# Attention's value product with its operands exchanged: values stationary, four heads in four column strips, output transposed

## The chip, the cores and the metric

The kernel runs on one core of one Trainium2 chip. The metric is the device time of one execution in microseconds (us): 1140.92 us is the median of three runs (1137.62 to 1145.13). The engines are named as in the profile: PE is TensorE's matmuls, PEld its weight loads, DVE is VectorE, ACT ScalarE, POOL GpSimd and SP SyncE.

## The reference, cut to what matters

Two layers, each an attention with context (16 batches of 128 tokens, width 256, 16 heads of 16) and a mixture of experts that picks 2 of 16 (layer 0) or 2 of 8 (layer 1). All values are float32. In each layer the attention is, for every batch:

```
qh = heads(norm(x) @ Wq + bq); kh = heads(ctx @ Wk + bk); vh = heads(ctx @ Wv + bv)
scores = q k^T / 4                 (causal mask in layer 0, masked query rows in layer 1)
attn   = softmax(scores)           (over the 128 keys)
out    = (attn @ vh) joined over heads, (128, 256)
x      = x + tanh(g) * (out @ Wo + bo)
```

The change is in `attn @ vh` and in what leads from it to `@ Wo`.

## The kernel before, in words

A tile is one batch: 128 tokens on the partitions. `attend(t)` is written out for every engine, and its order is the order of the engine's queue; counters (semaphores) tie the queues together, and `need(engine, counter, value)` is a wait. The work of several tiles is interleaved by hand: while tile t has its scores and its softmax, tile t-1 has its last value product, its division and its output projection, tile t+1 its projections, t-2 its second normalisation, t-3 to t-5 the routing of tokens to experts. The loop runs over 21 steps in each layer. The times of the stages are in the profile section.

The heads are taken in four groups g of four. For a group PE makes the scores of four heads at once (L1200, 128 x 512, in layer 0 with the causal mask added by L1204), DVE takes the row maxima (L806) and scales them (L811, L813), ACT takes the exponentials (L643), PE turns the four 128 x 128 blocks round (`turn_p`, L1212), ACT copies them to `probT` (L650), and PE multiplies them by the values (`weigh_v`, L1225). There each head is one matmul: its turned probabilities (128 keys x 128 queries) are the stationary operand, and the moving one has 17 columns: 16 values and a column of ones, which gives the row sum. So the 16 heads of a tile fill 272 columns of `bank[4]`, with the queries on the partitions.

`divide` on DVE takes the reciprocal of the 16 row sums (L834, 128 x 16) and multiplies (L837). `turn_o` on PE (L1238, two transposes) turns the result round, `oT_copy` on ACT (L656) brings it to SBUF, and `proj_o` (L1246) multiplies it by Wo. `residual` (L843, L845) adds it to x. In PE's order of a step stand: score 0; the transposes of the normalised x of t+1 (`turn_x`, L1154) and its value projection (L1180); routing (L1266 to L1277); `turn_p` 3 and `weigh_v` 2 of t-1; score 1; key projection (L1171); `turn_p` 0; `weigh_v` 3 of t-1; score 2; query projection (L1190); `turn_o` of t-1; `turn_p` 1, `weigh_v` 0, score 3; `proj_o` of t-1; `turn_p` 2, `weigh_v` 1. In DVE's order `divide` of t-1 stands between the maxima of group 1 and of group 2. POOL runs beside them: the power of the variance (L496), a part of the keys' blocks (L502), and the low parts of the experts' weights (L508), which are made ahead.

## Time and profile before

| | |
|---|---|
| median of three runs | 1140.92 us (1137.62 to 1145.13) |
| span of the profiled execution, first to last instruction | 1135.2 us |
| time of the profiled execution beside its span | not recorded apart; the span is 5.7 us under the median of the runs |
| attention of layer 0, first to last division | 39 to 274 us |
| attention of layer 1, first to last division | 483 to 776 us |
| experts, layer 0 / layer 1 | about 320 to 450 / about 800 to 1100 us |
| busy, whole span | PE 81%, PEld 64%, DVE 58%, ACT 49%, POOL 32% |

All times within the profile are from the span's start. A float32 matmul shows as two records, each with its own weight load: 1024 records at L1225 are 512 matmuls. The end of a matmul's record is modelled, and records overlap, so the pace is read from starts and from the chain of waits (the chain of work that ended last, followed back), not from busy time.

### The profile page before, as it was taken

Reading aid. Unit: us, or ns where it says so; the run is one execution under the profiler, and the core shown is the slowest. Engines: PE = TensorE matmul, PEld = TensorE weight load, DVE = VectorE, ACT = ScalarE, POOL = GpSimd, SP = SyncE. Lnnn points to the kernel's source line nnn. Section 1 sums busy time; section 2 is a strip of 40 time slices with the busy share of each in tenths; the row PEclk is TensorE's granted clock in tenths of the full one; section 3 lists DMA queues with packets and bytes.
Section 4 is the critical chain, followed back from the end, with each engine's and each line's share of the span. In section 5 each row is a group of like instructions: output and inputs, shape, how many; then the busy total and the mean of one; then the engine's idle time right before and its main releaser. Section 6 shows DMA issues by size and latency. Waiting matters only on the chain.

```text
span 1135.2 us, 26126 instructions
## 1 busy us (share of the span) xinstructions
PE 920.6 (81%) x7417; PEld 731.3 (64%) x7441; DVE 663.6 (58%) x1683; ACT 551.5 (49%) x1434; POOL 365.7 (32%) x359
## 2 busy tenths in 40 slices
PE   5998888996498885889888878885699999999920
PEld 3777676775486654567777657663577777777710
DVE  3678778786654444486777677675433334443323
ACT  3666656665234552575666566573233443333300
POOL 1335445454400001554564665565100000000046
PEclk9999899998699998797867787786799999999975
DMA  3121221221313443222222222120311111111034
GB/s 115 57 84 45 66 68 53 65 66 70 114 32 111 128 131 119 72 82 79 65 90 89 72 90 88 63 98 38 131 39 38 37 37 37 37 37 37 20 102 139
DMA packets 58764, 83.48 MB, mean 74 GB/s; under 512 B 8272, under 2 KB 49872, under 8 KB 58320
## 3 DMA queue, kind: packets, MB, share of 16 engines
q1 hardware_dynamic: 51984, 65.42, 18.0%
q0 software_dynamic: 6144, 16.79, 4.4%
q8 instruction: 32, 0.52, 0.2%
q10 hardware_dynamic: 576, 0.52, 0.1%
q14 instruction: 28, 0.23, 0.1%
HBM read 54.39 MB, written 28.31 MB: 73 GB/s over the span
## 4 chain that ended last, share of the span: by engine, by line
PE 56%; DVE 20%; issue 13%; POOL 5%; ACT 2%; DMA 2%; SPq 1%; another core or an unknown queue 1%; DVEq 0%; POOLq 0%; ACTq 0%
PE bank L1397 14%; PE bank L1410 13%; PE bank L1200 7%; PE bank L1225 5%; DVE work L795 5%; DVE work L806 3%; PE bank L1212 3%; POOL work L583 3%; PE bank L1385 2%; PE bank L1180 2%; PE bank L1171 2%; PE bank L1190 2%; PE bank L1154 2%; PE bank L1362 1%; PE bank L1277 1%
## 5 line engine op out<-in xcount | busy, mean ns | idle before, releaser
L1397 PE MATMUL bank<-work,arena 128*128 128x128 bf16 x2496 | 223.1, 224 | 0.0
L1397 PEld LDWEIGHTS bank<-work,arena 128*128 x2496 | 183.1, 98 | 28.8 <-issue 6.7
L1410 PE MATMUL bank<-arena,work 128*128 x1104 | 181.2, 275 | 6.5 <-DVE work L1112 1.1
L1200 PE MATMUL bank<-work 128*128 128x512 f32 x256 | 156.0, 694 | 1.4 <-ACT work L607 1.4
L643 ACT ACTIVATE work<-bank,work,qscale 128x128 f32<-128x128 f32 x256 | 96.8, 465 | 88.8 <-DVE work L813 79.0
L1225 PEld LDWEIGHTS bank<-work 128*128 128x128 f32 x1024 | 137.5, 209 | 0.6 <-ACT work L650 0.5
L806 DVE TENSOR_REDUCE work<-bank 128x4 f32<-128x512 f32 x128 | 88.2, 689 | 84.8 <-PE bank L1200 40.8
L1225 PE MATMUL bank<-work 128*128 128x17 f32 x1024 | 134.8, 265 | 0.4 <-ACT work L650 0.4
L583 POOL DMA_INDIRECT work<-y,slot x32 | 31.3, 977 | 298.0 <-DMA y<-work 288.6
L756 ACT ACTIVATE work<-bank,b 128x128 f32<-128x128 f32 x160 | 45.7, 368 | 164.1 <-PE bank L1397 164.1
L643 ACT ACTIVATE work<-bank,work 128x128 f32<-128x128 f32 x256 | 73.2, 371 | 73.4 <-DVE work L811 72.1
L508 POOL TENSOR_TENSOR arena<-work,arena 128x384 bf16<-128x384 f32 (+3 forms) x64 | 97.6, 1526 | 15.4 <-ACT arena L661 15.4
L1410 PEld LDWEIGHTS bank<-arena,work 128*128 128x128 bf16 x1104 | 78.9, 97 | 32.8 <-issue 14.1
L496 POOL TENSOR_TENSOR rstd<-vareps,mhalf 128x1 f32<-128x1 f32 x64 | 36.3, 567 | 177.4 <-DVE vareps L789 176.7
L1212 PE MATMUL bank<-cf,work 128*128 128x128 f32 x512 | 87.5, 299 | 0.2
L1154 PE MATMUL bank<-cf,work 128*128 128x128 f32 x128 | 31.4, 334 | 66.4 <-DVE work L795 66.4
L1132 DVE TENSOR_TENSOR work<-work 128x1024 bf16<-128x1024 f32 x40 | 49.0, 1225 | 61.6 <-ACT work L762 61.6
L533 POOL DMA_INDIRECT xg<-work,slot_pair x64 | 64.9, 1015 | 49.4 <-DVE slot_pair L911 36.5
L650 ACT ACTIVATE work<-bank 128x512 f32<-128x512 f32 x128 | 79.4, 621 | 2.8 <-PE bank L1212 2.7
L795 DVE TENSOR_SCALAR work<-x,meanvar,rstd 128x256 f32<-128x256 f32 (+1 forms) x64 | 69.1, 1080 | 10.0 <-POOL rstd L496 9.7
L1212 PEld LDWEIGHTS bank<-cf,work 128*128 128x128 f32 x512 | 70.6, 161 | 6.5 <-issue 2.0
L1154 PEld LDWEIGHTS bank<-cf,work 128*128 128x128 f32 x128 | 17.6, 175 | 88.1 <-issue 60.4
(134 smaller groups left out, 1542.6 us busy)
## 6 DMA issues: line engine op xcount, KB each, us to landing
work<-in_slab SPq DMA_DIRECT2D x32, 512.0 KB, 3.4
work<-xg SPq DMA_DIRECT2D x88, 128.0 KB, 2.0
y<-work SPq DMA_DIRECT2D x44, 256.0 KB, 2.1
work<-in_slab SPq DMA_DIRECT2D x32, 192.0 KB, 2.3
xg<-zeros SPq DMA_DIRECT2D x36, 128.0 KB, 1.8
work<-in_ctxT SPq DMA_DIRECT2D x32, 128.0 KB, 3.0
x<-in_x SPq DMA_DIRECT2D x16, 128.0 KB, 2.3
wat<-in_wat SPq DMA_DIRECT2D x2, 1024.0 KB, 5.0
```

Of the source, the lines that this page charges most:

```text
L508: pool.tensor_tensor(at(wlo[L], t.v)[:, c], stage[:, c], at(whi[L], t.v)[:, c], ALU.subtract).then_inc(lo_ok[half], 1)
L583: pool.indirect_dma_start(ylast[t % 4][c], None, y[1], bass.IndirectOffsetOnAxis(ap=slot[:, c, t:t + 1], axis=0)).then_inc(last_got[t % 4] ...
L643: i = act.activation(prob[g % 2][:, c], bank[g % 2][:, c], ACT.Exp, scale=scale, bias=shift[g % 2][:, h:h + 1])
L650: act.activation(probT[g % 2], bank[2 + g % 2][:], ACT.Copy).then_inc(pt_ok, 1)
L795: dve.tensor_scalar(xn[2 * w + t.par], at(x, t.v), meanvar[w][:, 0:1], rstd[w][:], ALU.subtract, ALU.mult).then_inc(xn_ok[w], 1)
L806: dve.tensor_reduce(rowmax[g % 2], bank[g % 2][:].rearrange("p (h t) -> p h t", h=GH), AX.X, ALU.max).then_inc(mx_ok, 1)
L1154: i = pe.transpose(bank[5][:, k * P:(k + 1) * P], xn[2 * w + t.par][:, k * P:(k + 1) * P], ident)
L1200: i = pe.matmul(bank[g % 2][:], qT[t.par][:, m * P:(m + 1) * P], kbd[:, m, 4 * (g % 2):4 * (g % 2) + 4, :].rearrange("p h t -> p (h t)"), ...
L1212: i = pe.transpose(bank[2 + g % 2][:, h * P:(h + 1) * P], prob[g % 2][:, h * P:(h + 1) * P], ident)
L1225: i = pe.matmul(bank[4][:, c:c + VW], probT[g % 2][:, h * P:(h + 1) * P], vaug[t.par][:, GH * g + h, :], start=True, stop=True)
L1397: i = pe.matmul(to, column(w, c, e, most, P), v, start=(k == 0 and q == 0), stop=(k == KT - 1 and q == 2))
L1410: i = pe.matmul(bank[6 + j.par][:, 0:D], a, column(w, c, e, most, D), start=(k == 0 and q == 0), stop=(k == nk - 1 and q == 2))
```

## The change

The value product's operands change places. For each head the stationary operand is now 32 columns wide: the head's 16 values and 16 zeros beside them. The moving operand is the head's turned probabilities, 128 columns. The four heads of a group go to four strips of 32 columns of the array, that is to PSUM partitions 0-31, 32-63, 64-95, 96-127. Groups 0 and 1 (and 2 and 3) share their strips: the first has its values in columns 0-15 of its strip and zeros in 16-31, the second the other way round, and the two are added up in PSUM. The layout of heads over groups changes to suit (`headrow`). Row sums come from four more matmuls of a group, with ones in place of the values, which give each sum 16 times, in columns 256 to 511 of `bank[4]`. So a group has 8 matmuls in place of 4.

The result has the head dimension on the partitions and the queries along the row, which is what `proj_o` needs. `turn_o` and `oT_copy` are gone. `divide` takes the reciprocal of 128 x 256 sums and multiplies 128 x 256, and writes `oT` itself. The waits on `oT_ok` become waits on `o_ok` and `xnT_ok`. `weigh_v` of group 0 waited for the division before (`o_ok`) and still does; `turn_o`, which waited for it earlier in the queue, is gone.

In PE's queue, the place where tile t-1 is turned and tile t starts its products (L1238 is `turn_o`, L1225 `weigh_v`), before:

```order
L1154 MATMUL bank<-cf,work 128x128 x2
L1200 MATMUL bank<-work 128x512
L1204 MATMUL bank<-cb 128x512
L1190 MATMUL bank<-work,wat 128x128 x4
L1238 MATMUL bank<-cf,work 128x128 x2
L1212 MATMUL bank<-cf,work 128x128 x4
L1225 MATMUL bank<-work 128x17 x4
L1200 MATMUL bank<-work 128x512
L1204 MATMUL bank<-cb 128x512
L1246 MATMUL bank<-wat,work 128x256 x2
```

and now (L1217 is `weigh_v`, other lines are moved by nine to twenty):

```order
L1145 MATMUL bank<-cf,work 128x128 x2
L1191 MATMUL bank<-work 128x512
L1195 MATMUL bank<-cb 128x512
L1181 MATMUL bank<-work,wat 128x128 x4
L1203 MATMUL bank<-cf,work 128x128 x4
L1217 MATMUL bank<-work 32x128 x4
L1217 MATMUL bank<-work,cf 32x128 x4
L1191 MATMUL bank<-work 128x512
L1195 MATMUL bank<-cb 128x512
L1226 MATMUL bank<-wat,work 128x256 x2
```

The two transposes are gone, and four matmuls of 17 columns have become eight of 128 columns, written to 32 partitions each.

In ACT's queue, the same step (L656 is `oT_copy`, L661 the high part of an expert's weights), before:

```order
L618 ACTIVATE arena<-bank 128x256
L619 ACTIVATE work<-bank 128x256
L661 ACTIVATE arena<-work 128x384
L656 ACTIVATE work<-bank 128x256
L643 ACTIVATE work<-bank,work 128x128 x4
L650 ACTIVATE work<-bank 128x512
```

and now:

```order
L617 ACTIVATE arena<-bank 128x256
L618 ACTIVATE work<-bank 128x256
L654 ACTIVATE arena<-work 128x384
L642 ACTIVATE work<-bank,work 128x128 x4
L649 ACTIVATE work<-bank 128x512
```

One copy, and its wait for PE, is gone from ACT; the rest keeps its place. DVE's order is the same, with wider operands in `divide`. The diff, cut to its core:

```diff
-VW = HD + 1
+VB = 3 * HD
...
-        causal = cb[:, 3 * P:]
+        onesv = cf[:, 224:224 + VB]
+        causal = cb[:, 3 * P:].unsqueeze(1).to_broadcast([P, GH, P])
...
-            def oT_copy(L, t):
-                n = t.plus(T * L)
-                need(act, pe_oT, n.v + 1)
-                need(act, pe_o, n.v)
-                act.activation(oT, bank[5][:, 0:KT * P], ACT.Copy).then_inc(oT_ok, 1)
-
...
-                dve.tensor_tensor(vaug[t.par][:, :, 0:HD], bank[7][:, 0:D].rearrange("p (h w) -> p h w", h=H),
-                                  bvo[:, 0, :].rearrange("p (h w) -> p h w", h=H), ALU.add).then_inc(v_ok, 1)
+                dve.tensor_tensor(vpad[t.par].rearrange("p (n c w) -> p n c w", c=3, w=HD)[:, :, 0:3:2, :],
+                                  bank[7][:, 0:D].rearrange("p (n c w) -> p n c w", c=2, w=HD),
+                                  bvo[:, 0, :].rearrange("p (n c w) -> p n c w", c=2, w=HD), ALU.add).then_inc(v_ok, 1)
 
             def divide(L, t):
                 n = t.plus(T * L)
-                o = bank[4][:, 0:H * VW].rearrange("p (h w) -> p h w", h=H)
                 need(dve, pe_pv, 4 * n.v + 4)
-                dve.reciprocal(rsum.unsqueeze(2), o[:, :, HD:VW]).then_inc(rs_ok, 1)
+                dve.reciprocal(rsum, bank[4][:, D:2 * D]).then_inc(rs_ok, 1)
                 need(dve, rs_ok, n.v + 1)
-                need(dve, pe_oT, n.v)
-                dve.tensor_tensor(on.rearrange("p (h w) -> p h w", h=H), o[:, :, 0:HD],
-                                  rsum.unsqueeze(2).to_broadcast([P, H, HD]), ALU.mult).then_inc(o_ok, 1)
+                need(dve, pe_o, n.v)
+                dve.tensor_tensor(oT, bank[4][:, 0:D], rsum, ALU.mult).then_inc(o_ok, 1)
...
-                for h in range(GH):
-                    c = (GH * g + h) * VW
-                    i = pe.matmul(bank[4][:, c:c + VW], probT[g % 2][:, h * P:(h + 1) * P], vaug[t.par][:, GH * g + h, :],
-                                  start=True, stop=True)
+                m, a = g // 2, g % 2
+                for c in range(2):
+                    out_cols = slice(c * D + m * P, c * D + (m + 1) * P)
+                    for h in range(GH):
+                        w = vpad[t.par][:, (m * GH + h) * VB:(m * GH + h + 1) * VB] if c == 0 else onesv
+                        i = pe.matmul(bank[4][32 * h:32 * h + 32, out_cols], w[:, a * HD:a * HD + 32], probT[g % 2][:, h * P:(h + 1) * P],
+                                      start=(g == 0 and c == 0), stop=(a == 1), skip_group_check=True)
                 i.then_inc(pe_pv, 1)
 
-            def turn_o(L, t):
+            def proj_o(L, t):
                 n = t.plus(T * L)
                 need(pe, o_ok, n.v + 1)
-
-                if inside(t, -1):
-                    need(pe, xnT_ok[1], n.v)
-                else:
-                    need(pe, xnT_ok[0], n.v + 3)
-                for k in range(KT):
-                    i = pe.transpose(bank[5][:, k * P:(k + 1) * P], on[:, k * P:(k + 1) * P], ident)
-                i.then_inc(pe_oT, 1)
-
-            def proj_o(L, t):
-                n = t.plus(T * L)
-                need(pe, oT_ok, n.v + 1)
                 need(pe, v_ok, n.v + 3 if inside(t, 2) else T * (L + 1))
...
                     if inside(t, 1):
-                        need(pe, oT_ok, t.plus(T * L - 1).v if inside(t, -2) else T * L)
+                        need(pe, xnT_ok[1], t.plus(T * L - 2).v if inside(t, -3) else T * L)
                         turn_x(0, L, t.plus(1))
...
-                    if inside(t, -1):
-                        turn_o(L, t.plus(-1))
```

## Rows read from the trace of the kernel before

**Rows 1.** The page: span; chain of waits by engine.

```profile
span 1135.2 us, 26126 instructions
...
PE 56%; DVE 20%; issue 13%; POOL 5%; ACT 2%; DMA 2%; SPq 1%; another core or an unknown queue 1%; DVEq 0%; POOLq 0%; ACTq 0%
```

**Rows 2.** Stretches: us, busy per engine (x instructions), granted clock, DMA.

```profile
39.00:81.60 42.60, 42.31 (x274) 33.65 (x279) 33.21 (x82) 27.68 (x87) 14.82 (x16) 1.00 0.24 72
81.60:274.50 192.90, 171.70 (x1090) 135.83 (x1107) 151.01 (x413) 123.58 (x374) 96.12 (x104) 0.96 0.19 59
483.00:776.40 293.40, 252.62 (x1325) 199.96 (x1325) 222.53 (x507) 183.63 (x446) 165.75 (x142) 0.80 0.24 80
```

**Rows 3.** Reciprocals (x) in the three stretches: us, busy, clock, DMA.

```profile
38.90:81.50 42.60, 0.77 (x3) 1.00 0.24 72
81.50:274.60 193.10, 3.27 (x13) 0.96 0.19 59
482.90:776.60 293.70, 4.08 (x16) 0.80 0.24 80
```

**Rows 4.** Chain of waits in the same three stretches: shares by line.

```profile
by line: PE bank L1200 24.2%; PE bank L1225 22.5%; PE bank L1212 12.5%; PE bank L1190 7.0%; PE bank L1171 7.0%; PE bank L1180 6.8%; PE bank L1246 6.5%; PE bank L1154 4.0%; PE bank L1204 3.5%; PE bank L1277 1.6%; PE bank L1238 1.5%; ACT work
...
by line: issue 14.6%; PE bank L1200 11.7%; DVE work L806 10.1%; PE bank L1225 7.5%; DVE work L795 5.7%; PE bank L1212 4.2%; DVE x L845 3.7%; DVE choice L897 3.7%; DVE choice L895 3.4%; another core or an unknown queue 3.1%; PE bank L1190 2.
...
by line: issue 20.6%; DVE work L795 13.0%; PE bank L1200 11.2%; PE bank L1225 9.7%; PE bank L1212 6.2%; DVE work L806 4.9%; PE bank L1180 4.9%; PE bank L1171 4.0%; PE bank L1154 2.7%; PE bank L1277 2.7%; PE bank L1190 2.1%; DVE work L820 1.
```

**Rows 5.** Chain, second layer, one tile: start us, us, what.

```profile
578.34 0.81 PE bank L1225 x8
...
579.18 0.27 DVE work L834
...
579.47 0.42 DVE work L837
...
586.63 2.07 DVE work L795
...
588.75 0.69 PE bank L1154 x2
...
593.11 1.52 PE bank L1225 x8
594.63 1.69 PE bank L1200 x2
```

**Rows 6.** Groups by line: busy us, mean ns; idle before, releaser.

```profile
L1225 PE MATMUL bank<-work 128*128 128x17 f32 x1024 | 134.8, 265 | 0.4 <-ACT work L650 0.4
...
L837 DVE TENSOR_TENSOR work<-bank,work 128x256 f32<-128x256 f32 x32 | 13.6, 424 | 1.1
...
L656 ACT ACTIVATE work<-bank 128x256 f32<-128x256 f32 x32 | 12.5, 392 | 19.9 <-PE bank L1238 19.8
...
L834 DVE RECIPROCAL work<-bank 128x16 f32<-128x16 f32 x32 | 8.1, 254 | 24.3 <-PE bank L1225 24.3
...
L867 DVE TENSOR_SCALAR choice<-bank 128x16 f32<-128x16 f32 x16 | 2.6, 165 | 2.2 <-PE bank L1277 2.2
```

**Rows 7.** One line, the transposes: duration ns min/median/max.

```profile
L1212 PE MATMUL bank<-cf,work x512: 272/273/454, 24.6 to 771.1; 128*128 128x128 f32 x171
```

**Rows 8.** TensorE in time, 16- and 32-column bf16 matmuls: start us, us.

```profile
91.78 0.17 PE L1267 MATMUL bank<-choice,cb 128*128 128x16 bf16 x1
...
91.81 0.17 PE L1268 MATMUL bank<-choice,cb 128*128 128x16 bf16 x1
```

**Rows 9.** Timeline, first layer: chain of four transposes; VectorE's waits.

```profile
80.19 0.60 PE L1212 MATMUL bank<-cf,work 128*128 128x128 f32 x4
...
82.97 0.69 DVE L806 TENSOR_REDUCE work<-bank 128x4 f32<-128x512 f32 x1 [0.63 <-PE bank L1204]
...
86.67 0.69 DVE L806 TENSOR_REDUCE work<-bank 128x4 f32<-128x512 f32 x1 [0.60 <-remote]
```

**Rows 10.** Timeline of VectorE, second layer, same tile.

```profile
584.51 2.21 DVE L813 TENSOR_SCALAR work<-work,qscale 128x4 f32<-128x4 f32 x1
```

36 lines of the change are left out of this document (16 added, 20 removed).

## The prediction, made before the change was run

> **What bounds the kernel now.** I read the page first, for the chain of waits as a whole [rows 1]: PE holds 56% of it and DVE 20%, in a span of 1135.2 us. The change touches only the two attention stages, so the chain is then asked stretch by stretch. I cut at the divisions of tiles: the first three of layer 0 (39 to 81.6 us), the other thirteen (81.6 to 274.5), and the sixteen of layer 1 (483 to 776.4) [rows 3]. The reader should see three different regimes. In the first PE never stops: it is busy for 42.31 of 42.60 us at a granted clock of 1.00 [rows 2], a tile takes 14.2 us, and `weigh_v` (L1225) is 22.5% of the chain [rows 4], 9.6 us, which is all its twelve groups. In the second a tile takes 14.8 us and DVE has parts of the chain; L1225 has 7.5%, 14.5 us. In the third a tile takes 18.3 us, DVE's normalisation L795 is among the first names, and L1225 has 9.7%, 28.5 us.
>
> One tile of layer 1 shows how they take turns [rows 5]: `weigh_v` of group 3 (0.81 us), then at once the reciprocal (0.27) and the product (0.42) of `divide`, then the maxima of groups 2 and 3 and the second normalisation on DVE until 588.7, and only then PE again, whose next `weigh_v` takes 1.52 us, because the clock granted after that stall is half of what it was: the mean of the stretch is 0.80 [rows 2]. So in layer 1 two of four groups and the whole of `divide` are on the path, every tile.
>
> **The change, part by part.**
>
> *The value product.* A group now costs 0.81 us on the chain for eight records [rows 5]: 17 columns are nothing, and eight loads of 128 columns are the price. After it a group has 16 records, each with a load of 32 columns and a stream of 128. A record of 128 float32 columns follows the next after 0.109 us: the four transposes at 80.19 last 0.60 us, of which the last takes 0.273, so three steps take 0.327 [rows 7, 9]. No row shows matmuls in column strips, so I bound it.
> - If strips don't overlap, 16 x 0.109 = 1.74 us.
> - If they overlap but matmuls start in order, the two records of one head follow each other in one strip, and only the second of a head and the first of the next run side by side: eight steps, 8 x 0.109 = 0.87 us.
> - If all four strips were always full, each strip has four records: 0.44 us.
>
> I take the second. To it come two costs that no row shows either. Each new head needs its weights before its first record: the nearest row is the pace of bf16 loads in front of narrow matmuls, 0.03 us [rows 8]; eight of them are 0.22, and the lower end is nothing. And the array goes from whole to strips and back. What a matmul lasts beyond its columns is 0.273 - 0.107 = 0.166 us [rows 7]; I charge it twice, 0.33, with nothing as the lower end. That gives 0.87 + 0.22 + 0.33 = 1.42 us, 75% more than 0.81. Applied to the chain's 9.6 + 14.5 + 28.5 = 52.6 us of L1225 it is **+39.5 us**. A share of the chain is used and not the 128 groups, since the others now lie beside DVE's work; in the first stretch there is no such cover and all are counted.
>
> The Trainium skill has a rule that speaks against the change here: "TensorEngine Tiling (Array Packing)", Key Properties, says that going from one tiling mode to another drains TensorE. It gives no duration. Without this seam the group above would be 1.09 us and the sum 21 us smaller.
>
> *The division.* The reciprocal goes from 16 to 256 columns. The row of 16 takes 254 ns, while an ordinary operation on 16 columns of a bank takes 165, and a product over 256 takes 424 [rows 6]. So an ordinary column costs (424 - 165) / 240 = 1.08 ns. The 89 ns that the reciprocal has more are either a fixed price, and then it takes 254 + 240 x 1.08 = 513 ns, or a price per column of 5.6 ns, and then 254 + 240 x 6.6 = 1.86 us. I take the second, since a start-up price of half an operation has no other row, and keep both. The added 1.60 us lie on the path in each of the 16 tiles of layer 1 (+25.6). In layer 0, DVE waits 0.63 us for PE before the maxima of group 2 and 0.60 before those of group 3 [rows 9], which hides most of it where PE leads; for thirteen tiles I take 8. Together **+33.6 us**. The product itself stays at 256 columns, 424 ns.
>
> The Trainium skill ("VectorE: DVE Perf Modes", First, the fixed hardware budget) says that the reciprocal is an iterative divide with a repeat count of 8. By it alone an estimate, at the 0.96 GHz of the same page, is 256 x 8 / 0.96 = 2.13 us and a start; the sum would be some 6 us larger.
>
> *What goes.* `turn_o` is 1.5% of the chain in the first stretch [rows 4], 0.6 us, and not seen in the others: **-0.6 us**. `oT_copy` is 0.39 us of ACT and a wait behind PE, 19.8 us in all [rows 6], but ACT's next work, the exponentials of group 2, waits for DVE's maxima as a rule, and those come later now. At nothing, for that cover; `proj_o` likewise starts one PE and one ACT step earlier after the division, which is itself later. A column of values is written with a gap, the same 256 columns; the wider constants and the memset come once. The mask is read with a repeat, same 512 columns. All at nothing.
>
> *Sum.* 39.5 + 33.6 - 0.6 = +72.5 us on 1135.2. The median of the runs lies 5.7 us above that span, so 1135.2 + 72.5 + 5.7 = **1213 us**.
>
> **The rivals.**
>
> *Strips one after another.* 1.74 + 0.33 = 2.07 us a group, 1.26 more, loads hidden under the streams. PE then needs 14.2 + 4 x 1.26 - 0.2 = 19.0 us for a tile, above the 14.2 and 14.8 of layer 0: +14.5 and +55 us. In layer 1 +156% of 28.5, and the division, +70. About 1280 us. For: each head comes as two records, no row shows overlap. Against: the partitions written are disjoint.
>
> *No seams and free loads.* 0.87 us a group: +4 us, with the division 1178. *A cheap reciprocal*, 0.51 us: 39.5 + 5.5 - 0.6, 1185.
>
> *Four strips at once, the rival on the other side.* A group at 0.44 us, -46% of 52.6: -24. This decides as long as the reciprocal adds less than 24.8 / 21 = 1.2 us (16 tiles of layer 1, and the 8 us of layer 0 counted as five), that is if it takes less than 1.45 us; with the fixed price the sum is -24.2 + 5.5 - 0.6, that is 1122 us, faster. With 1.86 us it is +9, 1150, within 1%. For it: the strips are independent in what they write. Against: the two records of a head share a strip.
> The Trainium skill ("TensorE: Matmul & The Clock Gate", Part 3) has three column strips measured at 2.38 times one; at that rate an estimate for four is 1.74 / 3.2 = 0.55 us a group.
>
> *The clock stays up in layer 1.* Streams of 128 columns in place of 17 leave the array less idle. A mean of 0.80 between levels of 1.2 and 2.4 GHz means 40% of 293 us at the lower one, 117 us; at full speed PE would do that work in half: at most -59 on +72.5, 1154 us. Against: the stall before the slow part waits for DVE (operations of 2.21 and 2.07 us in a row [rows 5, 10], where another over 256 columns takes 0.42 [rows 6]), and DVE gets longer.
>
> **How the numbers follow.** My forecast 38%, strips in a row 24%, no seams 12%, cheap reciprocal 8%, four at once 10% (6 faster, 4 same), clock 8% (3 faster through cheaper steps, 3 same, 2 slower). A measurement of this kernel tells 1% from no change. Slower by over 1%: 0.80; within: 0.08; faster: 0.12. The range reaches from the break-even of four strips to just above strips in a row, 1148 to 1285; below it lies the faster share, above it part of the second rival.
>
> **What would show it.** The eight matmuls of a group: start-to-start of records 16 times 0.11 us or half of that, and the gap before and after them; a group's time in the chain. The reciprocal's mean, 1.86, 2.2 or 0.5 us. The tile's pitch in the first stretch, 14.2 now: 16.3 by my sum, 19 in a row. The clock of layer 1. L1238's place taken by nothing. I am wrong if a group on the chain takes under 0.9 us or over 1.9, or if DVE's longer division shifts its collisions with POOL, which can give or take 2 us a tile.

## The result and the profile after

The changed kernel takes **1151.68 us** (median of 11 runs, 1146.87 to 1155.70) where the kernel before takes 1145.41 us (11 runs on the same chip, 1137.62 to 1151.00): a ratio of **1.0061, 95% interval 1.0034 to 1.0088**. That is 0.6% slower. The forecast was 6% slower, 1213 us; the measured time lies just inside its range, at the low end. Ratios here and below leave out the few runs that lie over 1.5% above the fastest of their kernel, so they can differ from the quotient of two medians (for before_stream_51 by 0.5%).

The page of the changed kernel, as [rows 1]:

```profile
span 1153.8 us, 27968 instructions
...
PE 48%; DVE 26%; issue 16%; POOL 5%; DMA 2%; ACT 2%; SPq 1%; DVEq 0%; POOLq 0%; ACTq 0%
```

The execution of [rows 1] was at the short end, its span 10 us under the median of the 11 runs of the same kernel, where the changed kernel's is 2 us over its own; so the two spans differ by 18.6 us and the medians by 6.3. I use spans only for shares and for single instructions, and medians for totals. What the page shows without that trouble is that PE fell from 56% of the chain to 48%, and DVE rose from 20% to 26%.

The same three stretches, cut at the same divisions as [rows 2], with the same columns:

```profile
39.40:83.60 44.20, 40.79 (x366) 26.94 (x366) 38.56 (x82) 26.66 (x84) 14.82 (x16) 1.00 0.22 66
83.60:284.80 201.20, 171.26 (x1466) 110.92 (x1466) 171.25 (x414) 120.17 (x363) 95.42 (x105) 0.94 0.18 57
493.60:794.10 300.50, 234.98 (x1774) 149.57 (x1774) 245.35 (x506) 179.21 (x431) 167.16 (x142) 0.84 0.24 78
```

In the first stretch PE's waits went from 0.3 us to 3.4, and DVE's work from 33 to 39. In layer 1 PE is busy for 18 us less, DVE for 23 us more, and now more than PE. The granted clock there is 0.84 where it was 0.80.

The chain of waits by line, as [rows 4], but asked of slightly shorter stretches: 39.4 to 82.4, 82.4 to 280.6 and 495.8 to 790.0 us (43.0, 198.2 and 294.2 us), which miss an end of each layer, the first reciprocal of layer 1 among it. L1217 is `weigh_v`, L825 the reciprocal, L786 the normalisation, L797 the maxima:

```profile
by line: issue 15.6%; DVE work L797 12.9%; DVE work L825 12.3%; DVE work L786 11.6%; DVE work L811 8.5%; PE bank L1217 5.7%; PE bank L1171 4.9%; PE bank L1191 4.9%; PE bank L1203 4.2%; PE bank L1162 4.1%; DVE stats L776 3.2%; DVE choice L88
...
by line: issue 16.8%; DVE work L797 11.5%; PE bank L1191 9.2%; DVE work L825 7.0%; DVE work L786 5.7%; PE bank L1217 4.5%; DVE x L835 4.2%; DVE choice L887 3.6%; DVE choice L885 3.3%; PE bank L1203 3.3%; PE bank L1162 3.0%; DVE stats L776 2
...
by line: issue 27.1%; DVE work L786 13.4%; PE bank L1191 6.7%; PE bank L1171 5.6%; PE bank L1217 5.2%; DVE work L797 5.2%; PE bank L1203 4.8%; DVE work L825 4.8%; DVE work L811 3.1%; PE bank L1162 3.0%; DVE choice L885 2.8%; PE bank L1257 2
```

Over the whole stretches (44.2, 201.2 and 300.5 us) `weigh_v` has 5.5, 4.5 and 5.1% of the chain and the reciprocal 12.0, 6.9 and 5.3%. So `weigh_v` holds 2.4 + 9.1 + 15.3 = 26.8 us, where it held 52.6, and the reciprocal 5.3 + 13.9 + 15.9 = 35.1 us, where it held 1.4. Minus 25.8 plus 33.7 is +7.9 us, close to the 6.3 between the medians. But the chain isn't a ledger: what leaves one line can return on another, and `weigh_v` lost its share in two ways. Its groups got shorter, and fewer of them are on the chain, 42 over the whole execution where there were 58; more of them now lie beside DVE's work. At the old count the shorter groups alone would be worth about 16 us (an estimate: 0.2 us for each of some 43 groups at full clock, 0.5 for each of some 15 at half).

The product and the division by line, as [rows 6] (busy us, mean ns; then idle time before them):

```profile
L1217 PE MATMUL bank<-work 128*32 128x128 f32 x1024 | 58.2, 302 | 2.0 <-DVE work L828 1.2 <-ACT work L649 0.7
L825 DVE RECIPROCAL work<-bank 128x256 f32<-128x256 f32 x32 | 56.1, 1753 | 14.0 <-PE bank L1217 13.9
L1217 PE MATMUL bank<-work,cf 128*32 128x128 f32 x1024 | 55.6, 292 | 0.0
...
L828 DVE TENSOR_TENSOR work<-bank,work 128x256 f32<-128x256 f32 x32 | 13.6, 425 | 1.1
```

One record of the product lasts some 300 ns where one lasted 265, and there are twice as many, yet their busy time is less: 114 us against 134.8. They overlap. PE in time, layer 0, one group:

```profile
64.52 0.63 PE L1203 MATMUL bank<-cf,work 128*128 128x128 f32 x4
65.08 0.43 PE L1217 MATMUL bank<-work 128*32 128x128 f32 x8
65.33 0.40 PE L1217 MATMUL bank<-work,cf 128*32 128x128 f32 x8
65.66 0.70 PE L1191 MATMUL bank<-work 128*128 128x512 f32 x1
```

All 16 records lie between 65.08 and 65.66, 0.58 us. Their starts, read from the records one by one, come in waves of four, 7 ns apart within a wave; from the first wave to the second it is 0.134 us, then 0.109 us twice. That is one record for each of the four strips, at the pace that one whole-array record has. The way in is longer than a step: the last transpose starts at 64.88, and the product 0.20 us later.

One tile of layer 1 on the chain, as [rows 5]:

```profile
582.76 0.41 PE bank L1145 x2
583.17 1.97 PE bank L1171 x4
585.14 0.66 PE bank L1257 x4
585.79 0.95 PE bank L1203 x4
586.74 1.01 PE bank L1217 x16
587.75 2.01 PE bank L1191 x2
589.76 1.02 PE bank L1162 x8
590.78 0.44 PE bank L1203 x4
591.22 0.62 PE bank L1217 x16
591.83 0.02 issue
591.86 1.77 DVE work L825
593.63 0.02 issue
593.65 0.42 DVE work L828
```

The turns are the same as in [rows 5]: PE at half the clock, PE at full clock up to the last group, then the division on DVE. The slow group takes 1.01 us where one took 1.52, the fast one 0.62 where one took 0.81, and the reciprocal 1.77 where it took 0.27.

### The profile page after: what moved, and what is told of

Same layout as the page of the kernel before. It is cut to its first block, busy times and chain, and to the rows that moved or that the text cites. A ratio compares the mean times of both kernels' runs of the same rounds, so it can differ in the third digit from the quotient of the medians.

```text
span 1153.8 us, 27968 instructions
## 1 busy us (share of the span) xinstructions
PE 896.3 (78%) x8400; PEld 643.3 (56%) x8401; DVE 718.0 (62%) x1683; ACT 541.3 (47%) x1402; POOL 366.0 (32%) x359
## 4 chain that ended last, share of the span: by engine, by line
PE 48%; DVE 26%; issue 16%; POOL 5%; DMA 2%; ACT 2%; SPq 1%; DVEq 0%; POOLq 0%; ACTq 0%
PE bank L1375 14%; PE bank L1388 13%; DVE work L786 5%; PE bank L1191 4%; DVE work L797 4%; DVE work L825 3%; PE bank L1217 3%; POOL work L582 3%; PE bank L1203 2%; PE bank L1171 2%; PE bank L1363 2%; PE bank L1162 2%; DVE work L811 2%; PE bank L1340 1%; DVE choice L885 1%
## 5 line engine op out<-in xcount | busy, mean ns | idle before, releaser
L1191 PE MATMUL bank<-work 128*128 128x512 f32 x256 | 159.3, 708 | 1.7 <-ACT work L606 1.4
L797 DVE TENSOR_REDUCE work<-bank 128x4 f32<-128x512 f32 x128 | 87.9, 687 | 62.0 <-PE bank L1191 33.5
L507 POOL TENSOR_TENSOR arena<-work,arena 128x384 bf16<-128x384 f32 (+3 forms) x64 | 97.0, 1515 | 14.7 <-ACT arena L654 14.7
L1388 PEld LDWEIGHTS bank<-arena,work 128*128 128x128 bf16 x1104 | 78.9, 97 | 33.6 <-issue 14.6
L786 DVE TENSOR_SCALAR work<-x,meanvar,rstd 128x256 f32<-128x256 f32 (+1 forms) x64 | 76.7, 1198 | 11.7 <-POOL rstd L495 11.7
L1145 PEld LDWEIGHTS bank<-cf,work 128*128 128x128 f32 x128 | 15.0, 158 | 123.4 <-issue 82.2
L1203 PEld LDWEIGHTS bank<-cf,work 128*128 128x128 f32 x512 | 68.8, 160 | 12.9 <-ACT work L642 8.2
L1092 DVE TENSOR_TENSOR work<-bank,work 128x256 f32<-128x256 f32 x40 | 17.0, 424 | 94.8 <-PE bank L1388 94.8
L512 POOL COPY slot_now<-slot 128x2 int32<-128x2 int32 (+1 forms) x16 | 2.9, 182 | 211.3 <-DMA y<-work 140.8
```

Of the source, the lines that this page charges most:

```text
L507: pool.tensor_tensor(at(wlo[L], t.v)[:, c], stage[:, c], at(whi[L], t.v)[:, c], ALU.subtract).then_inc(lo_ok[half], 1)
L786: dve.tensor_scalar(xn[2 * w + t.par], at(x, t.v), meanvar[w][:, 0:1], rstd[w][:], ALU.subtract, ALU.mult).then_inc(xn_ok[w], 1)
L797: dve.tensor_reduce(rowmax[g % 2], bank[g % 2][:].rearrange("p (h t) -> p h t", h=GH), AX.X, ALU.max).then_inc(mx_ok, 1)
L1191: i = pe.matmul(bank[g % 2][:], qT[t.par][:, m * P:(m + 1) * P], kbd[:, m, 4 * (g % 2):4 * (g % 2) + 4, :].rearrange("p h t -> p (h t)"), ...
L1203: i = pe.transpose(bank[2 + g % 2][:, h * P:(h + 1) * P], prob[g % 2][:, h * P:(h + 1) * P], ident)
L1388: i = pe.matmul(bank[6 + j.par][:, 0:D], a, column(w, c, e, most, D), start=(k == 0 and q == 0), stop=(k == nk - 1 and q == 2))
```

## The experiments

All totals are medians, ratios are against the kernel before on the same chip (its medians there are 1144.5 to 1148.3 us), with 95% intervals. Kernels that were run on different chips are best compared by their ratios.

| kernel | us | ratio | interval |
|---|---|---|---|
| changed kernel | 1151.7 | 1.0061 | 1.0034 to 1.0088 |
| after_narrow | 1112.8 | 0.9715 | 0.9678 to 0.9752 |
| before_wide | 1179.1 | 1.0291 | 1.0260 to 1.0321 |
| after_by_head | 1154.4 | 1.0083 | 1.0053 to 1.0113 |
| after_sums_by_exp | 1124.7 | 0.9825 | 0.9798 to 0.9853 |
| before_no_turn | 1144.7 | 0.9957 | 0.9929 to 0.9985 |
| after_one_strip | 1205.7 | 1.0501 | 1.0471 to 1.0532 |
| after_late_divide | 1179.4 | 1.0272 | 1.0242 to 1.0301 |
| after_no_ones | 1116.1 | 0.9723 | 0.9692 to 0.9753 |
| after_more_ones | 1120.1 | 0.9774 | 0.9730 to 0.9818 |
| before_half_product | 1112.7 | 0.9714 | 0.9672 to 0.9756 |
| before_long_stream | 1120.7 | 0.9771 | 0.9729 to 0.9812 |
| after_split_reciprocal | 1151.3 | 1.0027 | 1.0005 to 1.0048 |
| before_wide_long_stream | 1162.5 | 1.0134 | 1.0084 to 1.0184 |
| before_stream_51 | 1151.5 | 0.9980 | 0.9939 to 1.0022 |

### First: split the change at the reciprocal

**after_narrow**, the changed kernel with a reciprocal of 16 columns:

```diff
-                dve.reciprocal(rsum, bank[4][:, D:2 * D]).then_inc(rs_ok, 1)
+                dve.reciprocal(rsum[:, 0:H], bank[4][:, D:D + H]).then_inc(rs_ok, 1)
...
-                dve.tensor_tensor(oT, bank[4][:, 0:D], rsum, ALU.mult).then_inc(o_ok, 1)
+                dve.tensor_tensor(oT.rearrange("p (h w) -> p h w", h=H), bank[4][:, 0:D].rearrange("p (h w) -> p h w", h=H),
+                                  rsum[:, 0:H].unsqueeze(2).to_broadcast([P, H, HD]), ALU.mult).then_inc(o_ok, 1)
```

> The changed kernel with the reciprocal over 16 columns again, spread over the product; 15 of 16 columns of sums are not used, so the outputs are scaled by wrong sums. Theory A (the four strips gain about 0.15 us a group, and the wide reciprocal, 1.75 us, gives it back because it lies on the path in all of layer 1 and part of layer 0): 20 to 30 us less than the changed kernel, ratio to the kernel before 0.975 to 0.985. Rival B (the reciprocal is mostly hidden and the strips gain little or nothing on the path): at most 5 us less, ratio above 0.997.

**before_wide**, the kernel before with the sums' column read 16 times over, so that its reciprocal has 256 columns (it writes them over `on`, so the wait for the last use of `on` moves ahead of it):

```diff
-        rsum = part(H)
+        rsum = on
...
-                dve.reciprocal(rsum.unsqueeze(2), o[:, :, HD:VW]).then_inc(rs_ok, 1)
+                need(dve, pe_oT, n.v)
+                dve.reciprocal(rsum.rearrange("p (h w) -> p h w", h=H), o[:, :, HD:VW].to_broadcast([P, H, HD])).then_inc(rs_ok, 1)
```

> The kernel before with the reciprocal alone widened to 256 columns (each head's sum read 16 times); the outputs are unchanged. Theory A: each division longer by 1.50 us, on the path in about 21 of 32 tiles: +31 us, ratio 1.02 to 1.03. Rival B: hidden in both layers, ratio under 1.007.

**after_by_head**, the changed kernel with the two records' loops swapped, so that value and ones product of one head follow each other:

```diff
-                for c in range(2):
-                    for h in range(GH):
+                for h in range(GH):
+                    for c in range(2):
```

> The changed kernel with the eight matmuls of a group in another order: for each head its values, then its ones, so that neighbours in the queue write the same strip. If matmuls start in the order of the queue, only two strips run side by side: a group takes 8 or 9 steps of 0.109 us in place of 4 and two seams, +0.4 us or more a group, some 65 groups on the path: +25 us, ratio to before about 1.03. If the array sorts records by strip itself: no change against the changed kernel, ratio 1.006.

Measured: the wide reciprocal costs the kernel before 33 us (1179.1 against 1145.7), and taking it out of the changed one gives 39 (1151.7 to 1112.8). So everything else that the change does *gains* about 33 us. Where the 39 lie, the divisions of the traces say: layer 0 from 245.4 us to 232.3, layer 1 from 300.5 to 277.4, the other 3 us outside. Layer 1 of after_narrow:

```profile
479.30:756.70 277.40, 226.81 (x1775) 149.47 (x1775) 222.23 (x507) 178.16 (x431) 167.12 (x142) 0.85 0.26 85
```

The order of the heads makes next to no difference: a group at full clock takes 0.80 us from the last transpose to the next matmul where the changed kernel has 0.78, and the ratios, 1.0083 and 1.0061, lie within each other's intervals. The starts show why: after_by_head queues values and ones of each head in turn, but in its trace, in each of 124 groups, all eight records of the values start first, in waves of four, 13 to 14 ns apart, and the eight of the ones after them. So records start out of the queue's order, each strip at its own pace. Matmuls of one strip that stand next to each other in the queue don't hold up those of the others; that they would was my reason for charging eight steps.

### The overlap of the strips, and the ones

**after_one_strip** puts the four heads of a group in one strip:

```diff
-                    out_cols = slice(c * D + m * P, c * D + (m + 1) * P)
...
+                        a = h // 2
+                        out_cols = slice(c * D + h % 2 * P, c * D + (h % 2 + 1) * P)
...
-                        i = pe.matmul(bank[4][32 * h:32 * h + 32, out_cols], ...
-                                      start=(g == 0 and c == 0), stop=(a == 1), skip_group_check=True)
+                        i = pe.matmul(bank[4][32 * g:32 * g + 32, out_cols], ...
+                                      start=(h == 0 and c == 0), stop=(h > 1), skip_group_check=True)
```

> The changed kernel with all four heads of a group written into one column strip (strip g for group g) in place of one strip each: the same number of records, loads and columns, but nothing can run in another strip at the same time. The heads of a group land on each other, so what is computed is left wrong in that place. Theory A (the forecast failed because four strips really overlap, and without that overlap its rival 'strips one after another' would be the truth): the 16 records inside a group take 16 x 0.109 = 1.74 us in place of 0.37 at full clock, a group 2.1 to 2.2 us in place of 0.78; a tile of the first stretch grows by 4 x 1.37 = 5.5 us; total 1230 to 1290 us, ratio 1.07 to 1.13. Theory B (records of 128 columns follow each other fast whatever the strip, the strips add nothing): 1152 us as the changed kernel, ratio 1.00 to 1.01.

Measured: 1205.7 us, 54 more than the changed kernel, below the expected 1230. PE in time, layer 0, one group (L1218 is `weigh_v`):

```profile
60.15 0.60 PE L1203 MATMUL bank<-cf,work 128*128 128x128 f32 x4
60.68 1.06 PE L1218 MATMUL bank<-work 128*32 128x128 f32 x8
61.57 1.04 PE L1218 MATMUL bank<-work,cf 128*32 128x128 f32 x8
62.54 0.44 PE L1145 MATMUL bank<-cf,work 128*128 128x128 f32 x2
```

1.86 us for 16 records where four strips take 0.58, both with the way out of the product: 3.2 times. The Trainium skill ("TensorE: Matmul & The Clock Gate", Part 3) has three column strips at 2.38 times one, from which the prediction made an estimate of 3.2 for four, 0.55 us a group; the trace agrees. So the price inside a group was as theory A has it. But a tile of the first stretch took 18.4 us in place of 14.7, 3.7 more where 5.5 were expected, and the total fell short. Its stretches show why:

```profile
44.60:99.80 55.20, 55.20 (x367) 42.71 (x368) 37.07 (x82) 27.45 (x85) 14.81 (x16) 1.00 0.19 58
99.80:318.30 218.50, 216.34 (x1467) 167.28 (x1468) 167.49 (x412) 119.94 (x356) 94.92 (x104) 1.00 0.16 51
526.60:840.60 314.00, 283.81 (x1774) 216.72 (x1774) 244.66 (x506) 178.24 (x427) 166.61 (x142) 0.93 0.23 75
```

PE is busy for 48.8 us more in layer 1, yet the layer takes only 13.5 us more. Two things paid: PE stands idle for 30 us of it in place of 66, and the granted clock is 0.93 in place of 0.84, so that all PE work but the product takes 164 us in place of 193. The second was the first sign that I had left something out.

**after_no_ones**, after_narrow without the ones product (row sums aren't computed; the reciprocal takes 16 columns of the values' result instead):

```diff
-                for c in range(2):
+                for c in range(1):
```

> The changed kernel with the ones product left out (row sums are not computed) and a reciprocal of 16 columns whose result stands in for them: 8 records a group in place of 16, 4 strips. Compared with after_narrow (1112.8 us), the same with all 16 records. Theory A (inside a group four strips take their four records each, so half as many save two steps of the wave, 2 x 0.109 us = 0.2 us at full clock and 0.4 at half, times about 50 and 16 groups on the chain): 12 to 20 us less than after_narrow, 1093 to 1101 us, ratio 0.955 to 0.962. Theory B (a group is set by its seams and its handovers with ACT, not by its records): 1108 to 1113 us, ratio 0.968 to 0.972.

Measured 1116.1 against 1112.8 for after_narrow, ratios 0.9723 and 0.9715: leaving out the ones product gains nothing that can be told from noise. The expected saving of 12 to 20 us is refuted.

**before_no_turn**, the kernel before without the output's transposition:

```diff
-                    if inside(t, -1):
-                        oT_copy(L, t.plus(-1))
...
-                        turn_o(L, t.plus(-1))
...
-                    i = pe.matmul(bank[7][:, 0:D], oT[:, k * P:(k + 1) * P], wat[:, 3, k, :],
+                    i = pe.matmul(bank[7][:, 0:D], on[:, k * P:(k + 1) * P], wat[:, 3, k, :],
```

> The kernel before without turn_o and oT_copy: proj_o takes the untransposed product as its stationary operand (the output transposition is left out, everything else stays). The change without its wide reciprocal gains about 33 us over the kernel before (after_narrow: 0.9715), and this run asks how much of that is the removed turn. Theory A (the value product carries it, as its groups on the chain are 0.14 to 0.42 us shorter; the turn is worth the 0.6 us that the chain showed for it, plus little): ratio 0.995 to 1.000, less than 6 us. Theory B (the turn carries at least half, because its removal also removes a PE-ACT-PE handover between the division and proj_o and 20 us of ACT work): ratio 0.98 to 0.988, 14 to 23 us, of which most in layer 1. Theory C (all is the turn): 0.9715.

Measured: -0.43%, 5 us (2 to 8 by the interval). Theory A; the turn is not where the 33 us come from, though it is worth more than the 0.6 of the prediction.

### Where the reciprocal stands

**after_late_divide** moves `divide` behind the maxima of group 2:

```diff
-                    if inside(t, -1):
-                        divide(L, t.plus(-1))
                     if L and inside(t, 2):
                         combine(0, t.plus(2))
                     if inside(t, 0):
                         scores(L, t, 2)
+                    if inside(t, -1):
+                        divide(L, t.plus(-1))
```

> The changed kernel with the whole of divide (wide reciprocal and product) one place later in DVE's queue, behind the maxima of group 2 of the next tile. Theory A (the reciprocal's added 1.5 us are on the path because PE's scores and transposes of the next tile wait for maxima queued behind it; behind the maxima of group 2 part of it is covered): a gain of 5 to 15 us on the changed kernel, 1137 to 1147 us, ratio 0.992 to 1.001. Theory B (DVE is itself short of time in layer 1, wherever the reciprocal stands; only a shorter one helps): no change from 1152, ratio 1.005. A loss would mean that the first product of the next tile, which waits for bank 4 to be read, decides: then ratio over 1.01.

Measured 1179.4 us, 28 more than the changed kernel (24 by the ratios), as the last sentence had it. PE's first product of the next tile now waits for bank 4. In the trace:

```profile
L1217 PE MATMUL bank<-work 128*32 128x128 f32 x1024 | 57.7, 299 | 54.2 <-DVE work L828 49.8 <-issue 2.4 <-ACT work L649 1.9
```

It was 2.0 us of idle time in the changed kernel, and is 54.2. Both theories on covering the reciprocal stay undecided by this run, since it brought a wait of its own. In layer 1 the stretch between the divisions is shorter, 294.5 us in place of 300.5; layer 0 pays, 269.8 in place of 245.4.

**after_split_reciprocal** takes the first half of the columns earlier, behind the maxima of group 0:

```diff
+            def recip(L, t):
+                n = t.plus(T * L)
+                need(dve, pe_pv, 4 * n.v + 2)
+                dve.reciprocal(rsum[:, 0:P], bank[4][:, D:D + P]).then_inc(rs_ok, 1)
...
-                dve.reciprocal(rsum, bank[4][:, D:2 * D]).then_inc(rs_ok, 1)
+                dve.reciprocal(rsum[:, P:D], bank[4][:, D + P:2 * D]).then_inc(rs_ok, 1)
...
+                if g == 2:
+                    need(pe, rs_ok, 2 * n.v + 1)
```

> The changed kernel with the wide reciprocal in two halves of 128 columns: that of heads 0 to 7 right behind the maxima of group 0 of the next tile, when groups 0 and 1 are done, and PE's product of group 2 waits for it; that of heads 8 to 15 where the whole stood. DVE's work grows by one start, about 0.06 us a tile. Theory A (the reciprocal costs 39 us because it stands at the one place where PE has nothing ready; a half of it moved to where PE has work is free): a gain of 10 to 20 us on the changed kernel, 1132 to 1142 us, ratio 0.988 to 0.998. Theory B (in layer 1 DVE's sum of work sets the pace, so moving it changes little there, and group 2 now waits): 1148 to 1156 us, ratio 1.002 to 1.01.

Measured 1151.3 us, the changed kernel's time (by the ratios 0.3% less, at the edge of the noise). Two halves of 0.95 us are not much dearer than one of 1.75, but PE now waits for the first half, 18.7 us in all before group 2:

```profile
L1226 PE MATMUL bank<-work 128*32 128x128 f32 x1024 | 59.3, 307 | 18.7 <-DVE work L825 18.7
```

Theory B is nearer. Neither of the two places tried helps the long reciprocal; a shorter one does. The next kernel does that.

**after_sums_by_exp** makes the row sums where the exponentials are made, so that the reciprocal has 16 columns again, and lets ACT and PE spread and turn it (the ones product goes, and `divide` stands behind the maxima of group 2, as in after_late_divide):

```diff
-                    i = act.activation(prob[g % 2][:, c], bank[g % 2][:, c], ACT.Exp, scale=scale, bias=shift[g % 2][:, h:h + 1])
+                    i = act.activation(prob[g % 2][:, c], bank[g % 2][:, c], ACT.Exp, scale=scale, bias=shift[g % 2][:, h:h + 1],
+                                       accum_out=esum[t.par][:, k:k + 1])
...
+                dve.reciprocal(rinv[:], esum[t.par][:]).then_inc(rs_ok, 1)
...
+                act.activation(qT[t.par].rearrange("p (h w) -> p h w", h=H), rinv[:].unsqueeze(2).to_broadcast([P, H, HD]),
+                               ACT.Copy).then_inc(rw_ok, 1)
...
+                    i = pe.matmul(bank[4][:, D + m * P:D + (m + 1) * P], qT[t.par][:, m * P:(m + 1) * P], ident, ...
...
+                act.activation(rsum, bank[4][:, D:2 * D], ACT.Copy).then_inc(r_ok, 1)
```

> The changed kernel without the ones matmuls: the exponentials' own accumulator on ACT gives the 16 row sums with the queries on the partitions, DVE takes the reciprocal of 16 columns, ACT widens it to 256 columns, two PE matmuls with the identity turn it round and spread it, ACT copies it to SBUF, DVE multiplies after the maxima of group 2. Against the changed kernel: DVE -1.5 us a tile, PE -0.87 + 0.44, ACT +0.8 and whatever reading the accumulator 16 times costs. Theory A: DVE was the reason, so 15 to 30 us less, ratio to before 0.975 to 0.99, unless reading the accumulator adds over 0.1 us each (1.6 us a tile in ACT's chain), then about 1.0. Rival B: no gain, over 1.0.

Measured **1124.7 us, 1.75% faster than the kernel before**: a whole version that beats both. What it pays is on ACT, where these records stand:

```profile
L648 ACT ACTIVATION_READ_ACCUMULATOR work<-bank,work 128x1 f32 x256 | 55.1, 215 | 0.0
L648 ACT ACTIVATION_READ_ACCUMULATOR work<-bank,work,qscale 128x1 f32 x256 | 54.2, 212 | 0.0
...
L849 DVE RECIPROCAL rinv<-esum 128x16 f32<-128x16 f32 x32 | 8.0, 250 | 1.0 <-ACT work L648 0.9
```

### Where the 33 us come from

For the next runs I counted PE's time in the product, from a group's first record to the next other instruction: 109.7 us in the kernel before over both layers, 76.2 in the changed one.

**after_more_ones** is after_narrow with the ones product issued twice:

```diff
-                for c in range(2):
+                for c in (0, 1, 1):
```

> after_narrow with the ones product issued twice a group, 24 records in place of 16 (the row sums' columns are summed twice; as in after_narrow a column of 16 stands in for them). PE's time in the product, from the first record of a group to the next other instruction, was 109.7 us over both layers in the kernel before, 76.2 in the changed one, 75.0 in after_narrow, 45.9 in after_no_ones; here it should be about 104, nearly that of the kernel before. Theory A (PE's time in the product is what the change gained, 110 to 75 us, and below 75 other engines bound, as after_no_ones was no faster): the gain of after_narrow over before_no_turn, 28 us, is lost again at 0.6 to 0.85 of the added 29 us: 1130 to 1138 us, ratio 0.984 to 0.991. Theory B (the gain is not PE's time in the product, but something else that the turned product changed, such as the handovers around the division or DVE's reads of the bank): 1113 to 1120 us, ratio 0.969 to 0.975.

**before_half_product** is the kernel before with one product for each two heads (half of the weighing is left out):

```diff
-                for h in range(GH):
+                for h in range(0, GH, 2):
...
-                    i = pe.matmul(bank[4][:, c:c + VW], ..., vaug[t.par][:, GH * g + h, :],
+                    i = pe.matmul(bank[4][:, c:c + 2 * VW], ..., vaug[t.par][:, GH * g + h:GH * g + h + 2, :]...,
```

> The kernel before with two products of 34 columns a group in place of four of 17 (one head's probabilities stand in for two heads', so half of the heads' weighing is left out): half of the loads, 4 records a group in place of 8. PE's time in the product falls from 109.7 us to about 60. Theory A (product time on PE is on the path at 0.6 or more down to about 75 us, then hardly): a gain of 20 to 30 us, 1118 to 1128 us, ratio 0.974 to 0.983. Theory B (the product's time on PE is mostly covered by DVE and ACT, and the turned product gained elsewhere): less than 10 us, ratio 0.991 to 1.000.

Measured: taking product time off the kernel before gains 32 us (109.7 us of it became 52), but adding it to after_narrow (75 became 102) costs only 7, hardly more than the intervals of the two allow to tell from nothing. Theory A was right for one and wrong for the other. before and after_more_ones have nearly the same time in the product and differ by 24 us, of which the missing turn explains about 5. Their layer 1, after_more_ones:

```profile
482.20:761.10 278.90, 231.18 (x2254) 157.01 (x2254) 222.91 (x506) 177.94 (x431) 167.06 (x142) 0.89 0.26 84
```

The clock is 0.89, against 0.80 in [rows 2], and all PE work but the product takes 176 us there, where it took 192. So the form of the product, not its length, might be what matters. That can be tried in the old kernel.

**before_long_stream** is the kernel before, but each matmul of the product streams its 17 columns seven times over into 119 columns of the bank, and later heads overwrite the surplus:

```diff
-                    i = pe.matmul(bank[4][:, c:c + VW], probT[g % 2][:, h * P:(h + 1) * P], vaug[t.par][:, GH * g + h, :],
+                    i = pe.matmul(bank[4][:, c:c + 7 * VW].rearrange("p (r w) -> p r w", r=7), probT[g % 2][:, h * P:(h + 1) * P],
+                                  vaug[t.par][:, GH * g + h, :].unsqueeze(1).to_broadcast([P, 7, VW]),
```

> The kernel before with each of the value product's matmuls streaming its 17 columns seven times over (119 columns; the later heads overwrite the surplus, so the result is the same): the same eight loads of 128 columns a group, and records that keep the array streaming. Seen so far: before and after_more_ones have about the same PE time in the product (109.7 and 102.0 us), yet the second is 24 us faster, its granted clock in layer 1 is 0.89 in place of 0.80, and all other PE work there takes 176 us in place of 192. Theory A (the form of the product raises the clock: streams of 128 columns count where records of 17 columns behind a load of 128 do not): the clock of layer 1 rises to 0.86 to 0.90 and the other PE work there falls by 8 to 15 us; PE's time in the product grows from 109.7 to about 118 us (a record each 0.109 us in place of 0.10), so the whole is 1130 to 1145 us, ratio 0.988 to 1.000. Theory B (the clock of layer 1 follows how long DVE keeps PE waiting, not what PE's product looks like): clock 0.78 to 0.81 as before, and the longer product costs 4 to 8 us: 1148 to 1153, ratio 1.003 to 1.007.

Measured **1120.7 us, 2.3% faster**, for work that is thrown away, and beyond what either theory allowed. The three stretches:

```profile
41.30:84.00 42.70, 42.67 (x279) 33.78 (x278) 33.27 (x83) 27.68 (x88) 14.82 (x16) 1.00 0.23 71
84.00:276.40 192.40, 172.70 (x1107) 135.07 (x1106) 151.50 (x413) 123.47 (x373) 96.65 (x105) 0.97 0.19 59
485.90:754.70 268.80, 221.20 (x1324) 172.11 (x1322) 223.00 (x506) 181.30 (x445) 166.68 (x142) 0.94 0.27 87
```

Layer 0, where the clock was high already, is as before: the same 235 us. Layer 1 takes 268.8 us where it took 293.3 from its first division to its last, at a clock of 0.94: between levels of 1.2 and 2.4 GHz a mean of 0.80 over 293.3 us is 117 us at the lower one, and 0.94 over 268.8 is 32. All PE work but the product takes 161 us in place of 192; DVE has the same work (223.0 and 222.5), and PE stands idle no less: 47.6 us of the stretch, 40.7 before. (The two spans differ by only 17.9 us, since that of [rows 1] is short outside the attention stretches, 606.6 us against 613.4.) It is no chance of one trace: the clock over the whole execution is 0.907 in the median of its six runs, and 0.872 in the 17 of the kernel before beside them. And the longer records cost little while the clock is up:

```profile
61.10 1.05 PE L1225 MATMUL bank<-work 128*128 128x119 f32 x8
61.99 1.03 PE L1200 MATMUL bank<-work 128*128 128x512 f32 x2
```

Eight in 0.89 us, 0.81 before.

**before_stream_51** repeats the columns three times and not seven; **before_wide_long_stream** is before_long_stream with the reciprocal of before_wide.

The edit of the first, against before_long_stream:

```diff
-                    i = pe.matmul(bank[4][:, c:c + 7 * VW].rearrange("p (r w) -> p r w", r=7), ...
+                    i = pe.matmul(bank[4][:, c:c + 3 * VW].rearrange("p (r w) -> p r w", r=3), ...
```

> The kernel before with the 17 columns streamed three times over, 51 columns a record, where before_long_stream has 119. The load of 128 columns before each record stays, so a record's pace should be 0.10 to 0.109 us. Theory A (the clock follows the share of time in which columns stream, gradually): between the two, 1128 to 1142 us, ratio 0.984 to 0.996, clock of layer 1 0.84 to 0.90. Theory B (there is a step, and 51 columns are on the low side of it): 1144 to 1150, ratio 0.997 to 1.003. On its high side: 1118 to 1125, ratio 0.974 to 0.982.

> The kernel before with both additions: the reciprocal over 256 columns (before_wide, +33 us) and records of 119 columns (before_long_stream, -27 us). It has the old product, old division order, turn and copy. Theory A (the changed kernel is a higher clock minus a longer reciprocal; its shorter product and the missing turn add little): 1145 to 1158 us, ratio 0.998 to 1.010, the two effects add. Theory B (with the wide reciprocal PE waits so often that the clock stays low, and the changed kernel needed its shorter product as well): 1165 to 1180 us, ratio 1.016 to 1.029, clock of layer 1 under 0.82.

Layer 1 of before_stream_51, then of before_wide_long_stream:

```profile
486.90:787.10 300.20, 258.35 (x1324) 206.18 (x1323) 223.13 (x506) 184.08 (x445) 166.98 (x142) 0.78 0.24 79
```

```profile
496.00:794.80 298.80, 243.22 (x1325) 189.47 (x1323) 249.66 (x506) 184.02 (x445) 167.60 (x142) 0.86 0.24 78
```

With 51 columns nothing measurable changes, neither in time (ratio 0.9980) nor in clock; with 119 both do. With long streams the wide reciprocal costs 42 us (1120.7 to 1162.5), and of the wide kernel's 1179.1 us they take 17. The time lies above theory A's span and below theory B's; the clock of layer 1, 0.86, is above what B allows. So most of the 27 us between before_wide and the changed kernel can be had by the clock alone, in the kernel before. That the changed kernel gets as much from it isn't shown: its clock rises to 0.84, not to 0.86. What is left from 1162.5 to its 1151.7, 11 us (8 by the ratios), would have to come from the missing turn (5 us in before_no_turn) and the shorter product (109.7 to 76.2 us on PE); no run separates them there.

## Why the prediction was wrong

- **The value product, forecast +39.5 us, is the step that failed.** The prediction had a group grow from 0.81 to 1.42 us on the chain, "+75%". It shrank to 0.62 at full clock and from 1.52 to 1.01 at half, and the 52.6 us of the chain became 26.8. Of the three bounds for 16 records, 1.74, 0.87 and 0.44 us, I took the middle one, on the reason that matmuls start in order and the two records of a head share a strip. after_by_head refutes the reason, and the waves of four starts show the lowest bound. That rival, "four strips at once", had 10%. The sum also kept the number of groups on the chain; that fell from 58 to 42.
- **Loads (+0.22) and seams (+0.33).** The loads of 32 columns cost nothing that shows. The seams exist, and are smaller: 0.203 us between starts on either side of a group at full clock (medians over the groups), where a step is 0.109: 0.094 us each, 0.19 for both. The Trainium skill's rule ("TensorEngine Tiling (Array Packing)", Key Properties) that a change of mode drains the array agrees, at a third of a record's length.
- **The division, forecast +33.6 us, was right in sum**: +33 on the kernel before, 33.7 on the chain of the changed one, 39 as what after_narrow takes away. The choice between a fixed start and a price per column was right too: 1753 ns against 1.86 us. A column costs (1753 - 254) / 240 = 6.2 ns. The estimate of 2.13 us after the Trainium skill ("VectorE: DVE Perf Modes", First, the fixed hardware budget) was too high; the trace decides. In part the sum was luck, for "the whole of `divide` on the path, every tile" was read off one tile: on the chain before, the reciprocal stands in 5 of the 16 tiles of layer 1 and in none of layer 0. After the change it stands there in 10 tiles of layer 1 and 12 of layer 0, where I took sixteen and five. By after_narrow, layer 1 pays 23 us and layer 0 13, where I took 25.6 and 8. Both say that layer 0 was priced too low: DVE's waits of 0.6 us there hid less than I thought.
- **The turn, forecast -0.6 us**, is worth about 5. It was on the chain in the other stretches too, 1.5 us in each and 5.0 over the whole execution; I read only the first names of each list. ACT's copy and the hand-over behind it, taken at nothing, go as well; no run shows their share apart.
- **The clock, left out of the sum.** I had it as a rival with 8%, argued from the idle time of the array, and turned it down because DVE's stalls would stay. They did stay, and even grew, and the clock of layer 1 rose all the same, from 0.80 to 0.84 (over whole executions it is 0.885 in the median of the changed kernel's runs, and 0.871 to 0.873 in those of the kernel before that stand beside the experiments). before_long_stream shows that longer streams alone, with no less idle time, raise it to 0.94 in this kernel and are worth 27 us. The rival's 1154 us is near the 1151.7 measured, but by another way: it kept the forecast's dearer product and took the clock at its utmost. What the clock is worth in the changed kernel is known only from the kernel before with the wide reciprocal, 17 of 27 us at a clock somewhat higher.
- **Rivals.** "Strips one after another" was priced at 1280, and after_one_strip took 1206, since PE's idle time and its clock took up a large part. Its price had a slip as well: from the first division of a layer to the last there are 15 tiles and not 16, so a tile of the second stretch takes 16.1 us and one of layer 1 19.6, not 14.8 and 18.3. "Four strips at once" with the reciprocal at 1.86 us was 1150, within 1%, and is the nearest account: it has -24 for the product where the chain shows -25.8, and nothing for the clock.
- **The chances.** Those of the single cases add up to 0.84 slower, 0.07 within 1% and 0.09 faster; the 0.80, 0.08 and 0.12 behind them aren't their sums.

Not settled: how much of the last 11 us is the shorter product. before_half_product gains 32 us with a clock of 0.84 in layer 1 (0.80 before), so time and clock can't be held apart there.

## What to carry to other kernels

Where independent 32-column products like these go to the four column strips, count steps by the fullest strip, whatever the order in the queue, and charge a tenth of a microsecond at each change between strips and whole array. An operation priced per column must be kept narrow: spread its result, not its operand. And where the mean granted clock of a stretch is well below 1, PE's time can't be added up from records: try once what longer streams with no added matmul do to the clock, before shortening anything.

## What the runs showed that was not expected

- Streaming 119 columns in place of 17 behind the same loads: 1120.7 us for 1148.0; granted clock in layer 1 0.94 for 0.80. With 51 columns: no change, a ratio of 0.9980, and 0.78.
- Matmuls to different strips start out of the queue's order: with values and ones of each head in turn (after_by_head), all records of the values start before those of the ones.
- 27 us of added work on PE (after_more_ones) cost 7 us, and 29 us less (after_no_ones) gained nothing; the clock of layer 1 was 0.89 and 0.84, around the 0.85 of after_narrow.
- The reciprocal takes 254 ns for 16 columns (241 to 258), 953 for 128 and 1753 for 256 (1741 to 1759), and before_wide's 1754 for a column read 16 times over is the same as for 256 columns of their own.
- A sum taken along with an activation costs one more instruction on ACT, 212 to 215 ns, for each.
